# Four feature-major layer norms: mean subtracted by TensorE, squares split between ScalarE and GpSimd

## The reference

```python
def _layernorm(x, axis=-1, eps=1e-05):
    m = jnp.mean(x, axis=axis, keepdims=True)
    v = jnp.var(x, axis=axis, keepdims=True)
    return (x - m) / jnp.sqrt(v + eps)

x = x + _L0_attn_ref(_layernorm(x, axis=-1), ...)
x = x + _L0_ffn_ref(_layernorm(x, axis=-1), ...)
x = x + _L1_attn_ref(_layernorm(x, axis=-1), ...)
x = x + _L1_ffn_ref(_layernorm(x, axis=-1), ...)
```

## Time and profile before

| | us |
|---|---|
| median of three runs | 3838.73 |
| profiled execution, its own time | 3837.68 |
| its span, first to last instruction | 3835.2 |
| around the span | 2.5 |
| PE busy | 3693.5 (96%) |
| DVE busy | 3172.0 (83%) |
| ACT busy | 2826.4 (74%) |
| POOL busy | 2559.3 (67%) |
| granted clock of PE, mean | 0.994 |

### The profile page before, as it was taken

One profiled execution on the slowest core, in us unless ns is written; L12 is line 12 of the kernel. 1 busy time (PEld: TensorE's weight loads), 2 busy tenths in 40 slices (PEclk: granted clock), 3 DMA queues, 4 the chain that ended last, 5 costly groups with the idle time before them and its releaser, 6 DMA issues.

```text
span 3835.2 us, 154562 instructions
## 1 busy us (share of the span) xinstructions
PE 3693.5 (96%) x61387; PEld 2330.0 (61%) x61387; DVE 3172.0 (83%) x5421; ACT 2826.4 (74%) x6426; POOL 2559.3 (67%) x2466
## 2 busy tenths in 40 slices
PE   7998888999999999999999999999999999999999
PEld 4665555666646666556666556666466665566664
DVE  6886557999968999879999789998699997799996
ACT  6895456888848888658888478888488885688883
POOL 4553226888827888648888468887388885588882
PEclk9999999999999999999999999999999999999999
DMA  2000000000000000000000000000000000000000
GB/s 79 0 0 1 1 0 2 0 6 0 1 23 2 0 6 0 1 24 0 6 0 0 24 2 0 6 0 1 24 1 0 6 0 24 2 0 6 0 1 23
DMA packets 11668, 25.62 MB, mean 7 GB/s; under 512 B 2252, under 2 KB 6392, under 8 KB 10752
## 3 DMA queue, kind: packets, MB, share of 16 engines
q1 hardware_dynamic: 11520, 23.53, 1.7%
HBM read 21.43 MB, written 2.10 MB: 6 GB/s over the span
## 4 chain that ended last, share of the span: by engine, by line
PE 80%; DVE 2%; ACT 1%; issue 1%; POOL 1%; DVEq 0%; POOLq 0%; ACTq 0%
PE banks L1124 19%; PE banks L1105 18%; PE banks L1182 9%; PE banks L1163 9%; PE banks L1113 9%; PE banks L1084 6%; PE banks L1137 5%; PE banks L1093 3%; DVE w_t L1351 1%; PE banks L1214 1%; PE banks L1072 0%; PE banks L1064 0%; PE banks L1013 0%; POOL w_t L983 0%; DVE w_ss L1391 0%
## 5 line engine op out<-in xcount | busy, mean ns | idle before, releaser
L967 POOL TENSOR_TENSOR w_t<-w_t 128x512 f32<-128x512 f32 x768 | 980.8, 1287 | 374.4 <-DVE w_t L1351 280.8
L1351 DVE TENSOR_TENSOR w_t<-banks,w_tab 128x512 f32<-128x512 f32 x1512 | 943.4, 684 | 212.6 <-ACT w_sq L1505 204.9
L983 POOL TENSOR_TENSOR w_t<-w_t,w_rn 128x512 f32<-128x512 f32 x768 | 785.1, 1044 | 257.2 <-ACT w_rn L1547 249.5
L1105 PE MATMUL banks<-w_qk,w_xs 128*128 128x512 f32 x1512 | 812.3, 619 | 0.3
L1124 PE MATMUL banks<-w_vo,w_xs 128*32 128x256 f32 x12096 | 810.7, 385 | 0.8 <-issue 0.8
L1113 PEld LDWEIGHTS banks<-ident,w_t 128*128 128x128 f32 x3072 | 380.6, 140 | 417.7 <-issue 398.6
L1498 ACT ACTIVATE w_us<-banks 128x512 f32<-128x512 f32 x756 | 450.5, 596 | 160.8 <-PE banks L1124 156.3
L1113 PE MATMUL banks<-ident,w_t 128*128 128x128 f32 x3072 | 461.2, 273 | 12.5 <-POOL w_t L983 11.6
L1391 DVE TENSOR_REDUCE w_ss<-w_sq 128x16 f32<-128x1024 f32 x378 | 457.1, 1209 | 0.0
L1124 PEld LDWEIGHTS banks<-w_vo,w_xs 128*32 128x32 f32 x12096 | 316.0, 109 | 229.4 <-issue 65.1
L990 POOL TENSOR_TENSOR w_pr<-w_pr,w_rl 128x512 f32<-128x512 f32 x384 | 403.2, 1050 | 27.2 <-ACT w_rl L1552 27.2
(11 more groups left out here) (200 smaller groups left out, 5910.7 us busy)
## 6 DMA issues: line engine op xcount, KB each, us to landing
w_qk<-w_qk_in SPq DMA_DIRECT2D x6, 1024.0 KB, 4.8
w_v<-w_v_in SPq DMA_DIRECT2D x6, 512.0 KB, 5.7
w_o<-w_o_in SPq DMA_DIRECT2D x6, 512.0 KB, 6.4
m_w<-m_w_in SPq DMA_DIRECT2D x6, 342.0 KB
xT<-x_in SPq DMA_DIRECT2D x4, 512.0 KB, 5.4
out<-kept SPq DMA_DIRECT2D x8, 256.0 KB, 2.0
m_w<-m_w_in SPq DMA_DIRECT2D x6, 171.0 KB
r_tab<-r_tab_in SPq DMA_DIRECT2D x1, 512.0 KB
```

The lines of the kernel that those rows point to most:

```text
L967: nc.gpsimd.tensor_tensor(v1, v1, v2[:, :, ::-1, :], ALU.add).then_inc(S["added"], 1)
L983: nc.gpsimd.tensor_tensor(v1, v1, rn[j % 2][:, i * HALF:(i + 1) * HALF].unsqueeze(2) .broadcast_to([P, HALF, WD]), ALU.mult).then_inc(S["n ...
L1105: nc.tensor.matmul(banks[:, i, :], x[:], wqk[:, i * INNER + hh * C:i * INNER + (hh + 1) * C], start=True, stop=True).then_inc(S["qk"], 1)
L1351: nc.vector.tensor_tensor(dst[j % 2][:, i * C:(i + 1) * C].rearrange("p (h d) -> p h d", d=WD), src, tab[:, 2 * t + cs, i * WD:(i + 1) * W ...
```

## The change

The mean product is replaced by a product with the identity less the mean (`centre_w`, 127/128 on the diagonal and -1/128 elsewhere), which the host prepares and SP loads ahead of x. Its result in PSUM is already the centred chunk. DVE's subtraction goes. Five chunks (`DIRECT`: 0, 2, 4, 6, 7) are squared by ACT from PSUM, and DVE's last product reads them from PSUM. Three (`COPIED`: 1, 3, 5) are copied by DVE into `norm`, squared by POOL, and multiplied from there.

The centred chunks stay in PSUM, so the eight banks are shared: banks 0 to 4 hold centred chunks in turn (chunk c in bank c modulo 5) and banks 5 to 7 hold variances (c modulo 3). Chunk c's centring product, from c = 5 on, waits for the last product (`scaled`) of chunk c - 5; the variance product of c waits for the Ln (`logged`) of c - 3. In the fourth norm POOL makes the copies into `kept`, and the weight products go to banks 3, 4, 7 and 5 and wait for `scaled` of chunk 4 and for Ln of chunks 5 and 6.

The diff, for the first three norms (lines left out are the helpers that number semaphores and banks):

```diff
+        sp.dma_start(centre_w[:], h["centre_w"]).then_inc(sem("centre_loaded"), 16)
         for i, b in enumerate(range(0, B, 4)):
             sp.dma_start(xT[:, b:b + 4, PAD:], h["x"][:, b:b + 4, :]).then_inc(sem(f"x_loaded{i}"), 16)
...
         @block.tensor
         def _(pe):
+            def centre(c):
+                if c >= CENTRED:
+                    pe.wait_ge(scaled, passed(done + c + 1 - CENTRED))
+                nc.tensor.matmul(of(centred_bank(c)), centre_w[:], stream(c), start=True, stop=True).then_inc(centred, 1)
+
             def variance(c):
-                pe.wait_ge(squared, passed(done + c + 1))
-                nc.tensor.matmul(banks[:, c, :], mean_w[:], chunk(logv, c), start=True, stop=True).then_inc(var_in, 1)
+                if c in COPIED:
+                    pe.wait_ge(pooled, passed(in_copied(c)))
+                else:
+                    pe.wait_ge(squared, passed(in_direct(c)))
+                if c >= 8 - CENTRED:
+                    pe.wait_ge(logged, passed(done + c + 1 - (8 - CENTRED)))
+                nc.tensor.matmul(variance_bank(c), mean_w[:], chunk(logv, c), start=True, stop=True).then_inc(var_in, 1)
...
         @block.vector
...
             for c in range(NCH):
-                dve.wait_ge(mean_in, passed(done + c + 1))
-                nc.vector.tensor_tensor(of(chunk(norm, c)), stream(c), of(banks[:, c, :]), ALU.subtract)\
-                    .then_inc(centred, 1)
+                if c in COPIED:
+                    copy(c)
                 if c >= 2 * BEHIND:
                     scale(c - 2 * BEHIND)
...
         @block.scalar
...
+                if c in DIRECT:
+                    square(c)
+                if c >= BEHIND:
+                    invert(c - BEHIND)
+            for c in range(NCH - BEHIND, NCH):
+                invert(c)
```

More of the change, by code:

```diff
@@ L30 @@
 BEHIND = 2
+CENTRED = 5
+FUSED = (3, 4, 7, 5)
+COPIED = (1, 3, 5)
+DIRECT = (0, 2, 4, 6, 7)
 PER = CH // T
@@ L208, in _ @@
                     pe.wait_ge(sem(f"x_loaded{c // 2}"), 16)
[L209 removed]
+                centre(c)
                 if c >= BEHIND:
@@ L232, in _, with square, invert @@
         def _(pool):
-            for c in range(NCH):
-                pool.wait_ge(centred, passed(done + c + 1))
-                nc.gpsimd.tensor_tensor(chunk(logv, c), chunk(norm, c), chunk(norm, c), ALU.mult).then_inc(squared, 1)
+            for c in COPIED:
+                pool.wait_ge(copied, passed(in_copied(c)))
+                nc.gpsimd.tensor_tensor(chunk(logv, c), chunk(norm, c), chunk(norm, c), ALU.mult).then_inc(pooled, 1)
         @block.scalar
         def _(act):
+            def square(c):
+                act.wait_ge(centred, passed(done + c + 1))
+                nc.scalar.activation(chunk(logv, c), centred_bank(c), ACT.Square).then_inc(squared, 1)
+            def invert(c):
+                act.wait_ge(var_in, passed(done + c + 1))
+                nc.scalar.activation(chunk(logv, c), variance_bank(c), ACT.Ln, bias=eps_col[:]).then_inc(logged, 1)
+                act.wait_ge(logged, passed(done + c + 1))
+                nc.scalar.activation(chunk(logv, c), chunk(logv, c), ACT.Exp, scale=-0.5).then_inc(inverse, 1)
             nc.scalar.preload_act_table_set("natural_log_exp_and_others")
             for c in range(NCH):
[L241 to L244, removed]
+                if c in DIRECT:
[4 more added lines that the diff above has]
+                invert(c)
 @scoped
@@ L1657, in _, with copy @@
         def _(dve):
+            def copy(c):
+                dve.wait_ge(centred, passed(done + c + 1))
+                nc.vector.tensor_copy(chunk(norm, c), centred_bank(c)).then_inc(copied, 1)
             def scale(c):
                 dve.wait_ge(inverse, passed(done + c + 1))
-                dve.wait_ge(centred, passed(done + c + 1))
                 dve.wait_ge(moved, c + 1)
-                nc.vector.tensor_tensor(stream(c), of(chunk(norm, c)), of(chunk(logv, c)), ALU.mult).then_inc(scaled, 1)
+                if c in COPIED:
+                    dve.wait_ge(copied, passed(in_copied(c)))
+                    source = chunk(norm, c)
+                else:
+                    source = centred_bank(c)
+                nc.vector.tensor_tensor(stream(c), of(source), of(chunk(logv, c)), ALU.mult).then_inc(scaled, 1)
             dve.wait_ge(weights, 64)
@@ L1667, in _ @@
             for c in range(NCH):
-                dve.wait_ge(mean_in, passed(done + c + 1))
-                nc.vector.tensor_tensor(of(chunk(norm, c)), stream(c), of(banks[:, c, :]), ALU.subtract)\
-                    .then_inc(centred, 1)
-                nc.vector.tensor_copy(kept[:, c * PER:(c + 1) * PER, :], stream(c)).then_inc(moved, 1)
+                if c in COPIED:
+                    copy(c)
                 if c >= 2 * BEHIND:
```

105 lines of the change are left out of this document (78 added, 27 removed).

## The result

The changed kernel takes 3848.73 us (median of 14 runs, 3843.36 to 3852.26) against 3839.34 (14 runs, 3838.18 to 3844.16): ratio 1.0021, 95% interval 1.0013 to 1.0029. It is 9.4 us (0.2%) slower, and the forecast of 3839.6 with its range to 3845.0 missed it; the prediction had given a time above 3846.4 a chance of 0.06. The profiled execution took 3843.36 and its span is 3840.5, 5.3 us over the span of before; it happens to be the fastest of the fourteen, so the trace shows only somewhat more than half (5.7 us against the profiled execution of before) of what the medians show.

A forecast was written before the change was run, and what follows sets the result against it. PE, busy 96% of the span, was taken to bound the kernel, with ACT's tail binding the changed norms; 1.35 + 0.68 - 1.17 = +0.86 us gave 3838.5 for the profiled execution, 3839.6 for the median, range 3834.5 to 3845.0.

The forecast's parts named there:

- first variance product to end: Inside a norm: from the first variance product to the norm's end 15.02 us, where the third norm took 14.36.
- the wait for chunk 1: Inside a norm: PE's centring product of chunk 6 waits 0.69 us for DVE's last product of chunk 1.
- the fourth norm: Norm four: its end comes at 601.79 instead of 602.96 us, -1.17, because DVE had fallen behind there.
- the rival in which PE stays the bound: Norms: DVE and ACT keep up, first variance product to end 13.41 us, total 3833.4; chance 0.09.
- DVE reading PSUM costs nothing: DVE's last product in the norms: reading the centred chunk from PSUM adds nothing; the skill's 0.065 us was not added.
- The start: Head of norm one: matrix load ahead of x +0.52 us, one more semaphore at most 0.07; shift bounds 0 and 1.2.
- The sum ahead of the layers: All four norms with the start: 1.35 + 0.68 - 1.17 = +0.86 us.
- The end of the first norm: Norm one: +0.76 us within the norm, together with the later start +1.35.
- the next two norms: Norms two and three: +0.34 us each, +0.68 for both; head and tail gain less than c6 and ACT take.
- The step that failed: Six layers: the change does not touch them, so only the four norms were priced.
- the bound of 2 to 3 us: Six layers: a start moved by 1 us may shift each by up to 1 either way, some 2 to 3 over six.
- The rival through PE's clock: Stages after norms and layer transitions: longer PE idle brings five more 1.2 GHz stretches, 8.3 us, total 3847.9; chance 0.06.

The follow-up runs named there:

- fewer waits: Changed kernel without PE's waits that other waits imply (on Ln; matrix and x share semaphores): 3840.93 us, ratio 1.0005.
- the same with 24: Changed kernel without its implied waits, with 24 empty semaphore instructions on PE in the first norm: 3846.41 us, ratio 1.0020.
- new order: Changed kernel without implied waits, with DVE's last product of chunk 1 ahead of its copy of chunk 5: 3839.80 us, ratio 0.9999.
- 20 on SP: Kernel before with 20 semaphore instructions on SP ahead of the first norm's loads, so work starts later: 3840.20 us, ratio 1.0004.
- the pair with and without: Changed kernel without implied waits, with and without 24 empty instructions on PE in the first norm: 3846.41 against 3840.93 us.
- a shift of 36: Kernel before with 36 empty semaphore instructions on PE in the first norm: 3854.87 us, ratio 1.0037.
- a shift of 256: PE's layer code 256 instructions later: changed kernel with 232 more, 3844.68 us; kernel before with 256 more, 3850.02 us.

## Why the prediction was wrong

- *Inside the norms it was right.* In the changed kernel's trace, first variance product to end 15.02 forecast, 14.99 and 15.05 measured; the wait for chunk 1 0.69 forecast, 0.53 measured; the fourth norm, its first instruction to the layers, 21.86 us where it was 22.95, forecast -1.17. ACT is never idle in the tail, as said, and the rival in which PE stays the bound is out.
- *DVE reading PSUM costs nothing, as taken.* In the changed kernel DVE's product takes a median of 691 ns with its operand in PSUM and 693 with both in SBUF. Of the 0.065 us more that the prediction took from the Trainium skill (VectorE: DVE Perf Modes, the TRN2 errata) for a PSUM source, no sign is seen.
- *The start was undersized*: 1.14 us instead of 0.59. SP's issue of x moved by 0.48, as forecast, but x then took 4.74 us to release PE instead of 4.08, where I had allowed 0.2 for sharing. In three other traces with the matrix ahead of x on SP (fewer waits, the same with 24, new order) the first product comes at 12.69 to 12.87, 0.8 to 0.9 later than before, so the size varies. With the matrix on another queue nothing of it is left.
- *The sum ahead of the layers came near by luck*: +0.86 forecast, -0.10 measured at the layers' first instruction. The end of the first norm is 1.95 later (forecast 1.35), the next two norms are 0.28 and 0.29 longer (0.34 each), the fourth 1.09 shorter (1.17), in all +1.4. The experts and the retention, which the change doesn't touch, came 0.5 and 1.0 us shorter in this trace, for a reason that no run isolates.
- *The step that failed* is the first one, that the change "does not touch" the six layers, and the bound of 2 to 3 us for them by a start that has moved. The start's phase costs nothing (20 on SP). What the change touched there is PE's code, by 24 instructions ahead of it, and that was worth 6.4 us by itself (3.9 of them in the layers of its trace) and 5.5 in the pair with and without (5.4 in the layers). In the changed kernel's own trace the layers are 5.5 us longer, with 5.4 us more of issue, beyond the 2 to 3 that the bound allowed. The count could have been made beforehand from the diff, and the rows for it were in the trace of before: the instruction queue with its 107 packets, and PE's 4.2 us of issue on L1163. The wait added to each variance product has no term in the sum; it is satisfied in time, and it still had a price, elsewhere.
- *The rival through PE's clock came nearest in time* (3847.9), but for a reason that isn't the one: in the profiled execution the granted clock over the layers is the same as before, 3.5 us lost in either. As a consequence of the code's stops it is real, shown at a shift of 36. At 24 it shows at one place in the kernel with fewer waits (a stop of 1.66, a wait of 1.13, then four MATMULs in 3.00 us), but that trace lacks the stretch of before at 3217 us, so its sum is no larger. The slower runs of the changed kernel, 3849 to 3852, come with a mean clock of 0.992 to 0.993, and its fastest with 0.994.

*What stays open*: about 4 us of the 9.4, of which the clock may be a part. The profiled execution has 5.5 in the layers; the median run isn't traced. The waits alone (24 back into the kernel without them) make 5.5 of the 7.8 us that taking them out had given; the other 2.3 are within what two medians of kernels with a spread of 6 to 9 us can differ by, and weren't separated. That the period is 256 is shown by the places of the stops in two kernels and by the length of the layers in one of them; a gain in the whole time isn't shown, since the added instructions don't all fit into waits. Why the sum of the stops rises with the shift, and what shifts between 36 and 256 do, wasn't measured.

## What to carry to other kernels

Where much of PE's code is written out ahead of or between loops and PE is the bound, the number of PE's instructions ahead of it is a variable of its own: count it before and after a change, semaphore waits included, and where it moves expect several us that have nothing to do with the change (here 24 and 36 made the kernel slower, and no shift made it faster). Test a small change of such a kernel with the same number of empty instructions at the same place, before its gain or loss is put down to what it does. A wait that another wait already implies was not free here even where it never waited: merge semaphores and drop implied waits first.

## What the runs showed of the hardware

- PE's program comes in packets of 16 KB, one for mostly 220 to 300 records of the layers' written-out parts (median 255), and at some of them PE stands still for 0.6 to 2 us until 2.2 to 2.9 us after the packet began. The places of these stops move with the code, to the instruction, and come back at a shift of 256. 12, 24 and 36 empty instructions of 0.15 us each, run while PE waited for x (the last of the 36 beyond that), made the kernel slower by 1.7 (not clear of noise), 6.4 and 15.0 us; 20 on ACT or SP made no difference.
- A second wait of an instruction shows as a record of its own, as the 24 of this change do. The Trainium skill, Perfetto Trace Analysis, section Identifying Dependency Chains, says that semaphore instructions may be inserted ahead of an instruction that waits on several engines; the trace agrees, with 24 more of them on PE.
- The head of the second norm runs at either level of the clock, by small differences ahead of it. With 24 empty instructions on PE in the first norm, 300 us earlier, six MATMULs take 4.51 us, where they took 2.81 both before and in the changed kernel; with 20 on SP they take 4.48:

```profile
341.41 4.51 PE L220 MATMUL banks<-xT,mean_w 128*128 128x512 f32 x6 [0.78 <-PEq L300]
```
